# A local attention whose mask moves from TensorE to ScalarE, in a loop that is written out

## The reference

```python
def local_attention(q, k, v):          # windows of w = 32 tokens, each sees itself and the one before
    mask = (it < jb) | (it > jb + w) | (jb == -1)
    sim = jnp.einsum('bhwie,bhwje->bhwij', bq, bk2) * QK_SCALE
    sim = jnp.where(mask, -jnp.finfo(sim.dtype).max, sim)
    attn = jax.nn.softmax(sim, -1)
    out = jnp.einsum('bhwij,bhwje->bhwie', attn, bv2)
...
for i in range(DEPTH):
    x = attn_layer(shift_tokens(x), Wqkv[i], q_scale[i], k_scale[i], Wo[i]) + x
    x = ffn_layer(shift_tokens(x), ln_g[i], ln_b[i], W1[i], b1[i], W2[i], b2[i]) + x
```

## Time and profile before

| | |
|---|---|
| median of 3 runs | 4816.22 us (4808.3 to 4830.12) |
| profiled execution | 4819.65 us, span 4817.9 us |
| PE busy | 4398.4 us, 91% of the span |
| DVE / ACT / POOL busy | 3142.6 / 2723.2 / 2626.5 us |
| first q projection of the transformer stage | 227.1 us after the start |
| its last round of the loop starts | 3277.6 us after the start |
| granted TensorE clock over the span | 0.959 |

### The profile page before, as it was taken

The page is one execution under the profiler, slowest core; times in us unless marked ns, Lnnn a source line. Parts: engine busy times, 40 slices in busy tenths (PEclk is TensorE's granted clock), DMA queues, the critical chain, the costliest instruction groups (busy, mean ns, idle before and its releaser), DMA issues. The chain is left out here.

```text
span 4817.9 us, 164830 instructions
## 1 busy us (share of the span) xinstructions
PE 4398.4 (91%) x72648; PEld 2863.6 (59%) x72648; DVE 3142.6 (65%) x4111; ACT 2723.2 (57%) x3930; POOL 2626.5 (55%) x1467
## 2 busy tenths in 40 slices
PE   7489999999999999999999999999984999788878
PEld 5256666666666666666666666666652555344435
DVE  3477676767667666667666676766743443599974
ACT  4246665656666565566656665665652444577743
POOL 0266665666666665666666665666632212477752
PEclk8599999999999999999999999999995999799989
DMA  2100001000100001100010001000001000211100
GB/s 55 51 11 16 19 20 37 20 20 18 30 24 25 18 18 33 27 20 15 20 37 23 17 20 29 24 24 18 19 14 33 1 1 1 87 76 71 71 34 16
DMA packets 184442, 134.16 MB, mean 28 GB/s; under 512 B 122296, under 2 KB 170433, under 8 KB 181633
## 3 DMA queue, kind: packets, MB, share of 16 engines
q1 hardware_dynamic: 183681, 122.99, 8.5%
HBM read 68.50 MB, written 4.03 MB: 15 GB/s over the span
## 5 line engine op out<-in xcount | busy, mean ns | idle before, releaser
L1005 POOL TENSOR_TENSOR tf_qk<-tf_qk,tf_rot 128x1024 f32<-128x1024 f32 x384 | 908.9, 2367 | 1221.8 <-DVE tf_rot L1388 1221.8
L1071 PE MATMUL tf_psum<-tf_Wqkv,tf_xsT 128*128 128x512 f32 x1536 | 749.6, 611 | 66.9 <-issue 46.5
L1012 POOL TENSOR_TENSOR tf_qk<-tf_qk,tf_rn 128x1024 f32<-128x1024 f32 x384 | 724.3, 1913 | 53.5 <-ACT tf_rn L1271 53.4
L1264 ACT ACTIVATE tf_sq<-tf_psum 128x1024 f32<-128x1024 f32 x384 | 393.4, 1025 | 533.7 <-DVE tf_rot L1388 533.7
L1384 DVE TENSOR_TENSOR tf_qk<-tf_psum,tf_table 128x1024 f32<-128x1024 f32 x384 | 467.4, 1217 | 265.3 <-PE tf_psum L1071 264.6
L1144 PE MATMUL tf_psum<-tf_probT,tf_V 32*64 32x64 f32 (+1 forms) x27648 | 494.1, 219 | 7.0 <-issue 6.6
L1071 PEld LDWEIGHTS tf_psum<-tf_Wqkv,tf_xsT 128*128 128x128 f32 x1536 | 273.4, 193 | 350.1 <-issue 339.3
L1394 DVE TENSOR_REDUCE tf_ss<-tf_sq 128x16 f32<-128x1024 f32 x384 | 457.6, 1192 | 21.3 <-ACT tf_sq L1264 21.3
L1144 PEld LDWEIGHTS tf_psum<-tf_probT,tf_V 32*64 32x64 f32 x27648 | 443.4, 133 | 45.7 <-issue 40.4
L1388 DVE TENSOR_TENSOR tf_rot<-tf_psum,tf_table 128x1024 f32<-128x1024 f32 x384 | 465.7, 1213 | 0.0
L1053 PE MATMUL tf_psum<-ident,tf_qk 128*128 128x128 f32 x3072 | 408.5, 276 | 3.4 <-ACT tf_qT L1283 2.4
(11 more groups left out here) (319 smaller groups left out, 7483.8 us busy)
## 6 DMA issues: line engine op xcount, KB each, us to landing
mb_Csb<-mb_kept SPq DMA_DIRECT2D x16, 2048.0 KB, 7.1
tf_zr<-z SPq DMA_DIRECT2D x96, 128.0 KB, 2.7
z<-tf_z SPq DMA_DIRECT2D x48, 256.0 KB, 2.5
tf_Wqkv<-in_Wqkv_split SPq DMA_DIRECT2D x18, 512.0 KB, 3.7
tf_zu<-z SPq DMA_DIRECT2D x97, 64.0 KB
tf_zu<-z SPq DMA_DIRECT2D x97, 63.5 KB
tf_zsh<-tf_z SPq DMA_DIRECT2D x96, 64.0 KB
tf_zsh<-tf_z SPq DMA_DIRECT2D x96, 63.5 KB
```

The costliest lines, as they stand in the source:

```text
L1005: nc.gpsimd.tensor_tensor(v, v, rot[:, kind, :], ALU.add).then_inc(added.sem, 1)
L1012: nc.gpsimd.tensor_tensor(v, v, rn[:, t, HEADS * kind:HEADS * (kind + 1)].unsqueeze(2) .to_broadcast([P, HEADS, HD]), ALU.mult).then_inc(n ...
L1071: last = nc.tensor.matmul(proj[:, half, :], xsT[:, step.unit(0), WIN + t * P:WIN + (t + 1) * P], Wqkv[:, c:c + 512], start=True, stop=True)
L1264: nc.scalar.activation(sq[:, kind, :], flat2(proj), ACT.Square).then_inc(squared.sem, 1)
```

## The change

Two things are changed. `all_steps` no longer makes a loop: all 208 steps are written out on each of the four compute engines, and semaphore targets become constants. And the mask goes into the score banks another way: after ACT has copied V out of them, a new ACT instruction (`open_scores`) writes the mask in float32 into all 1024 columns, and the score matmuls (start=False) are added to it. TensorE's mask matmuls stay for the very first tile alone.

```diff
-def all_steps(engine, body):
-    for k in range(LOOP):
-        body(Step(0, k))
-    with engine.Fori(1, ROUNDS) as I:
-        for k in range(LOOP):
-            body(Step(I, k))
-    for k in range(LOOP):
-        body(Step(ROUNDS, k))
+def all_steps(body):
+    for n in range((ROUNDS + 1) * LOOP):
+        body(Step(n // LOOP, n % LOOP))
...
                 pe.wait_ge(copied, place(step.before(), "k") + 2)
-                pe.wait_ge(v_kept.sem, v_kept.at(tau - 1, 1))
-                for odd in range(2):
+                pe.wait_ge(opened.sem, opened.at(tau - 1, 1))
+                for odd in range(2 if tau == 0 else 0):
                     nc.tensor.matmul(score[:, odd, :], identb[:, :], mask[:, t:t + 1, :].to_broadcast([P, PAIRS, HD]),
...
+            def open_scores(step):
+
+                tau, t = step.tile(2), step.t(1)
+                act.wait_ge(v_kept.sem, v_kept.at(tau, 1))
+                nc.scalar.activation(score.rearrange("p b (a e) -> p (b a) e", e=HD),
+                                     mask32[:, t:t + 1, :].to_broadcast([P, HEADS, HD]), ACT.Copy).then_inc(opened.sem, 1)
...
                 if step.has(2):
                     keep_v(step)
+                    open_scores(step)
                 if step.has_input():
                     copy_input(place(step, "input"), (step.k // 2 + 1) % 4)
```

More of the change, by code:

```diff
@@ L708, in has @@
     def has(self, lag):
-        return not isinstance(self.I, int) or 0 <= self.tile(lag) < TILES
+        return 0 <= self.tile(lag) < TILES
     def has_input(self):
-        return self.k % 2 == 1 and (not isinstance(self.I, int) or self.tile(0) < TILES)
+        return self.k % 2 == 1 and (self.tile(0) < TILES)
     def pair(self):
@@ L718, in has_pair @@
     def has_pair(self):
-        return not isinstance(self.I, int) or 0 <= self.pair() < UNITS // 2
+        return 0 <= self.pair() < UNITS // 2
     def before(self):
@@ L761, in place @@
 def place(step, name):
-    if isinstance(step.I, int) and step.I == 0:
+    if step.I == 0:
         return FIRST_FILLS[step.k, name]
-    if isinstance(step.I, int) and step.I == ROUNDS:
+    if step.I == ROUNDS:
         return LAST_FILLS[step.k, name]
     return (step.I - 1) * ROUND_FILLS + (LOOP_START + LOOP_FILLS[step.k, name])
-def all_steps(engine, body):
-    for k in range(LOOP):
-        body(Step(0, k))
-    with engine.Fori(1, ROUNDS) as I:
-        for k in range(LOOP):
-            body(Step(I, k))
-    for k in range(LOOP):
-        body(Step(ROUNDS, k))
+def all_steps(body):
+    for n in range((ROUNDS + 1) * LOOP):
+        body(Step(n // LOOP, n % LOOP))
 def transformer_stage(k, z):
@@ L850, in transformer_stage @@
         v_done, v_kept, pv_done = ev("v_done"), ev("v_kept"), ev("pv_done", 2)
-        scored, maxed, centred, exped, den_sum, den_inv, prob_ready, o_copied, out_done, z_added = (
-            ev(n) for n in "scored maxed centred exped den_sum den_inv prob_ready o_copied out_done z_added".split())
+        scored, opened, maxed, centred, exped, den_sum, den_inv, prob_ready, o_copied, out_done, z_added = (
+            ev(n) for n in "scored opened maxed centred exped den_sum den_inv prob_ready o_copied out_done z_added".split())
         ln_stats, ln_moments, ln_logged, ln_rstd, xn_centred, xn_ready = (
@@ L1042, in body @@
                     weigh(step)
-            all_steps(pool, body)
+            all_steps(body)
         @block.tensor
@@ L1065, in project @@
                     pe.wait_ge(e.sem, e.at(step.I * (LOOP // 2) + step.k // 2, 1))
-                    if kind == 0 and not (isinstance(step.I, int) and tau == 0):
+                    if kind == 0 and tau:
                         pe.wait_ge(copied, place(step.before(), "input") + 2)
@@ L1247, in _ @@
             pe.wait_ge(copied, 2)
-            all_steps(pe, body)
+            all_steps(body)
         @block.scalar
         def _(act):
-            for e in (squared, logged, rn_ready, v_kept, exped, o_copied, ln_logged, ln_rstd, gelued):
+            for e in (squared, logged, rn_ready, v_kept, opened, exped, o_copied, ln_logged, ln_rstd, gelued):
                 e.start(act)
@@ L1356, in _ @@
             copy_input(0, 0)
-            all_steps(act, body)
+            all_steps(body)
         @block.vector
@@ L1483, in body @@
                     add_hidden(step.pair(), step.k // 4 % 2)
-            all_steps(dve, body)
+            all_steps(body)
 QH, QD = 16, 8
```

## The result

| | median us (range) | ratio to the kernel before, 95% interval |
|---|---|---|
| before, beside it | 4813.45 (4808.3 to 4830.12) | |
| changed | 4875.16 (4867.0 to 4878.3) | 1.0121 [1.0097, 1.0146] |

What follows compares the result with a forecast made beforehand. TensorE, 91% busy, was taken to bound the kernel, except kind 3, bound by a chain through gelu and DVE. 4819.65 + 19 (mask) - 44 (writing out) + 5 (stalls) = 4800, as median 4797 us; range 4752 to 4843.

Steps and rivals of the forecast that it cites:

- The branch: At the loop's ten returns TensorE stands still; writing the steps out was to gain 5 x 3.95 + 5 x 4.9 = 44 us.
- The new instruction: ScalarE's 1024-column mask write into PSUM was taken at 1.08 us plus 0.03 us wait, 1.11 us a step.
- The chain through gelu: Kinds 1 to 3: mask write delays input copy, gelu 1 and `attend` by 1.4 us; +64 us, +19 with 45 gained.
- I cost them at nothing: Register instructions for semaphore targets in the loop: dropping them was to gain 0 us, as sequencers compute under running instructions.
- The failed step: TensorE's instruction stalls away from branches, some 40 us in 11 rounds: written out, +5 us, between -40 and +35.
- It just fits, with no slack.: Kind 1: ScalarE's mask opens the banks at 1545.25 us, TensorE could start scores at 1545.3, so no delay.
- The third: Rival, straight code still starves: stalls of 1.2 us in every kind 1 step and some others, +30 us, 4827 us; chance 0.12.
- The first: Rival, ScalarE's new instruction is dearer: 14 us per 0.1 us beyond 1.08; 4841 us, at the upper bound 4905; chance 0.15.
- the fifth: Rival, writing out does not gain its 44 us, as TensorE waits for weights or DVE instead: 4841 us; chance 0.10.
- the fourth: Rival, straight code never starves TensorE of instructions: 40 + 5 us more gained, 4752 us; chance 0.10.
- the second: Rival, the chain through gelu does not bind, so all 192 tiles gain 0.45 us: 4691 us; chance 0.08.

Runs made afterwards that it cites:

- e2: The changed kernel, still written out, with the mask put back on TensorE and ScalarE's mask instruction dropped: 4778.79 us, 0.9914 of the kernel before.
- e5: As e4, but TensorE writes all masks; in kinds 0 and 1 it first waits for an equal-sized ScalarE write into unused SBUF: 4821.32 us, 1.0008.
- e6: As e4, without ScalarE's mask instruction and the wait for it, so kinds 0 and 1 have no mask (time only): 4737.81 us, 0.9832.
- e4: The changed kernel with ScalarE's mask only for scores of kinds 0 and 1, TensorE's for kinds 2 and 3: 4778.33 us, 0.9933.
- e7: The changed kernel with ScalarE's mask write placed behind gelu 0 and gelu 1 in steps of kinds 1 and 2: 4918.39 us, 1.0212.
- e8: As e4, but ScalarE writes the mask for kind 0 alone, TensorE for the other kinds: 4763.42 us, 0.9892.
- e9: As e8, but VectorE writes the mask for kind 2; ScalarE keeps kind 0, TensorE kinds 1 and 3: 4749.57 us, 0.986.
- e3: The changed kernel with 64 one-column products of zeros (128 instructions) added on TensorE at the start of the stage: 4876.56 us, 1.0123.

## Why the prediction was wrong

- **The branch.** Forecast 44 us. Measured 53.9 - 16.6 = 37.3 at the returns, and 1.11 us stay at the change of layer shown, where 1.2 was expected. In e2 it is 53.9 - 11.3 = 42.6. The term holds. What stands behind the standstill is more than the forecast saw. The projections of the earlier trace rows that "come slowly" come at half the clock:

```profile
1042.00:1044.00 2.00, 2.00 (x23) 0.46 (x29) 1.32 (x7) 0.50 (x2) 0.00 (x0) 0.50 0.02 5
```

  So it is at eight of the ten returns. At the other two (2160.86 and 3277.61) the clock stays full and the projection takes 1.98 us, but TensorE then stalls twice more, by 0.25 and 1.0 us, and the two steps lose 4.3 and 4.0 us all the same. What the clock by itself adds to a return is not separated.
- **The new instruction.** Forecast 1.08 + 0.03 us; measured 1.028, and it starts 1.05 us after V's copy starts, 0.03 after that ends. Into SBUF, from the same source, ScalarE takes 1.057 us (e5's instruction), 3% more.
- **The chain through gelu.** Right in its place and nearly in its size. Forecast: the input copy late by 0.6 us, gelu 1 by 1.4, a group longer by 1.4 - 2 x 0.45 = 0.5. Measured 0.96. In kind 0 the gain is 0.27 us instead of 0.45, though the scores start 1.81 us after the q projection, where they started 2.24 us after it: 0.43 us. The mask before started 1.72 us after it, so 0.09 us of gap stay ahead of the first score. From the start of kind 1 to `attend` in kind 3 it is 16.98 + 16.45 + 12.28 = 45.71 us, where before it was 16.72 + 16.54 + 11.23 = 44.49: +1.22, forecast 1.4 - 0.45 = 0.95. Of the 0.46 us that the forecast of the group falls short, 0.19 belong to the next point. In rounds 1 to 11 the group's part is 41 us, where 19 stood in the sum.
- **"I cost them at nothing": the register instructions.** The first 16 steps, which have none, were "as long as in the loop to within 0.1 us", and I dropped that difference. e2 shows it: its kinds 0, 1 and 2 take 14.71, 16.78 and 16.60 us where the loop has 14.65, 16.72 and 16.54, its group 67.43 against 67.24. Over 44 groups that is +8 us. That there is nothing to gain by dropping them the trace of the kernel before shows: in rounds 1 to 11 they take 34 ns each on TensorE, and 1597 of 1637 run while a product or a weight load runs; on ScalarE it is 1377 of 1409, with 36 ns each.
- **The failed step: "Away from branches TensorE also waits for instructions ... I take +5 us, between -40 and +35."** Measured +36.5 in rounds 1 to 11, past the end of that range, and part of the 12.8 us of the first round is of the same sort (three waits for `opened`, and from its seventh step on the granted clock is 0.50 for 10 us where the kernel before has none). The reason that I gave for harder hits, the missing slow masks, is right in size, 0.35 to 0.5 us a stall (e6 against e2, e4 against e5), and the smaller part. The step failed because I took it for the only one, and so put the whole term at +5. What makes a stall longer by another 1.0 to 1.1 us is a wait that I had already looked at: "It just fits, with no slack." I asked only whether TensorE would stand still there, and it doesn't in the undisturbed step. But it cannot issue past the wait before 1420.92 either, and then 64 small products (256 records with their weight loads) follow which it issues within 1.5 us. Before, the wait was over at 1544.13, and the mask began at 1545.23, so there was 1.1 us to run ahead in the earlier trace rows. In kind 3, too, the time before the need fell from 2.38 to 1.41 us, and 15 stalls stand in its scores where there was none.
- **The rivals.** The third, straight code still starves, came nearest in its cause, with 4827 us, yet it counted stalls of 1.2 us; they are 2.1 to 2.7 in kind 1 of the changed kernel, with the low clock behind some. The first (a dearer instruction) and the fifth (no gain from writing out) lie nearer in number, with 4841 us, and are refuted, by 1.028 us and by the 37.3 us at the returns. So are the fourth (never starves), by the 61.9 us ahead of the scores, and the second (the chain does not bind), by the group of 68.20 us.

With the measured terms the sum is 4819.65 + 41 - 37 + 36.5 + 12.8 + 6 - 1.8 = 4877 us, the profiled time. Of these +36.5 and +12.8 were put at 5, and +41 at 19: 44 and 22 us of the 77 that the sum of 4800 us falls short. The range was too narrow because the largest unknown, bounded by -40 and +35, was entered at its middle, and the first round was not in the sum at all.

**What is shown and what is argued.** Shown: stalls lie at a fixed count modulo 256, and the steps that they hit move with added instructions; the later wait makes them longer by 1.0 to 1.1 us, the missing masks by 0.35 to 0.5. Output weights slowed by the clock came only in kernels with the late wait. The low clock itself did not: the kernel before has 44 us of it in rounds 1 to 11, 34 of them at returns of the loop, against 31 in the changed kernel, 20 in e4, 34 in e5, 109 in e7, none in e2 and 3 in e6, e8 and e9. Argued, an estimate from the records at which kind 1's stalls begin (165 to 171): that TensorE's instruction stream asks for the next block some 170 records ahead of a block's end, so that an end nearer than that behind a wait is asked for only when the wait is passed, and the wait's delay is added to the stall. Two rows speak for it: no end within the first 164 records of kind 1's scores stalls TensorE in any written-out kernel, and the stall is as long at record 178 as at 255 (2.18 and 2.26 us in the changed kernel), which would not be so if the fetch began at the wait itself. No view shows when a fetch is asked for. Not tried: ScalarE's extra instruction without the wait for it. VectorE's in e9 goes with longer stalls as well, and e5's writes to SBUF, so neither ScalarE nor PSUM is needed for them. Open is what makes the 6 us behind the last projection: 9.7 us are added in the last steps of the transformer, and the stages behind it are 3.4 shorter. e2 has 16 there, of which 10 lie in stages where nothing is changed but the code ahead, with 242 us at the low clock instead of 215 behind the last projection; why the clock falls more often is not shown.

## What to carry to other kernels

A wait that is over just in time was not free here: behind it stood a run of 64 small products, and where a block of TensorE's instructions ended in the later part of that run, the stall was 1.83 us instead of 0.84 (e5 and e2), without masks 2.33 instead of 1.19 (e4 and e6), at times with a granted clock of 0.50 behind it. So before a step is handed to an idle engine, ask by how much each wait now comes before the need, not only whether it delays; the same move made only where 2.55 us (kind 0 under `narrow`) or 1.38 us (kind 2 on VectorE) are left turned 1.2% lost into 1.4% gained, and even at 1.38 us the stalls came back and took some 10 us. Compare stalls one by one, too, and not only their sum: two kernels with other instruction counts have other numbers of them. Two parts of a change that touch the same stalls don't add: here -36 and +68 made +60.

## What the runs showed of the hardware

- After stalls of 1.8 to 2.7 us (once, at 2115 us of the changed kernel, 1.13) on a TensorE that was otherwise busy the granted clock was 0.50 in some cases (1426.00 to 1428.00) and stayed 1.00 in others: after the stall of 2.32 us that ended at 1569.88 the output weights took their 1.95 us. The output weights of six steps of the changed kernel were slowed, by 6.3 us together.
- A return of the loop that is no change of layer cost TensorE 3.95 to 4.8 us where the granted clock fell to 0.50 behind it (three returns) and 4.0 and 4.3 us where it stayed full (two).
- TensorE stalled in straight-line code too, at places whose count of records leaves 193 or 194 modulo 256 in all written-out kernels (one in e3 195), by 2.05 to 2.67 us in kind 1's scores of the changed kernel and 0.56 to 1.12 in e2's. The steps that were hit came in stretches of rounds that go with the number of records in a group modulo 256 (11 over: every 23 groups; 27 over: every nine or ten). In kind 1 an end within the first 164 records of the scores went with no stall in any written-out kernel. Shifting the start by half a block moved the stretches and left the total (4876.56 against 4875.16 us).
- Steps that are written out, with constant targets, were 0.06 us longer in three kinds of four than those of the loop, though each lost its register instructions. On TensorE the trace has 35 separate semaphore instructions a group against 18 in the loop; that these are the cause was not tried.
- VectorE wrote 1024 columns of float32 from SBUF into PSUM in 1.228 us (e9), ScalarE in 1.028 (the changed kernel).
